# Norms of one group's queries and keys as two 64-column products, their inverse root on 256 columns, spread to 128 partitions by transfers

## The reference, cut to what matters

```python
def l2norm(t):
    return t / jnp.maximum(jnp.linalg.norm(t, axis=-1, keepdims=True), 1e-12)

def attn_layer(x, Wqkv, qs, ksc, Wo):
    qkv = x @ Wqkv
    q, k, v = ...                       # 16 heads of 64
    q = l2norm(q) * qs
    k = l2norm(k) * ksc
    q = q * cos * scale + rotate_half(q) * sin * scale
    k = k * cos * inv + rotate_half(k) * sin * inv
    out = local_attention(q, k, v)      # windows of 32 tokens, each sees itself and the one before
    return out @ Wo

for i in range(DEPTH):                  # DEPTH = 6
    x = attn_layer(shift_tokens(x), ...) + x
    x = ffn_layer(shift_tokens(x), ...) + x
```

## Time and profile before

| | |
|---|---|
| median of three runs | 1870.31 us |
| the profiled execution: its time | 1873.87 us |
| the profiled execution: its span | 1872.1 us |
| TensorE matmul busy | 1808.1 us (97%) |
| VectorE busy | 1535.6 us (82%) |
| ScalarE busy | 1456.2 us (78%) |
| GpSimd busy | 1359.4 us (73%) |
| granted TensorE clock, mean | 0.998 |

### The profile page before, as it was taken

How to read it: one execution, slowest core, us unless ns; L and a number is a source line. 1 busy time by engine, 2 the same in 40 slices (tenths; PEclk the granted TensorE clock), 3 DMA queues, 4 the chain that set the end, 5 groups by cost and what they waited for, 6 DMA issues and landing times.

```text
span 1872.1 us, 67927 instructions
## 1 busy us (share of the span) xinstructions
PE 1808.1 (97%) x26763; PEld 1370.4 (73%) x26763; DVE 1535.6 (82%) x3002; ACT 1456.2 (78%) x2976; POOL 1359.4 (73%) x1165
## 2 busy tenths in 40 slices
PE   6999998999999999999999999999999999999997
PEld 4777776777777777777777777777777777777774
DVE  5776777788889888888888888888888888888886
ACT  5766665678798888888887888778878878887884
POOL 3010023889889888888888898888888888888880
PEclk9999999999999999999999999999999999999999
DMA  3000001344343444334444434443344434444342
GB/s 111 1 1 0 0 25 28 91 114 116 104 110 100 112 113 111 97 103 110 114 112 104 105 102 115 113 107 101 103 106 122 112 98 103 111 104 103 98 103 69
DMA packets 200545, 171.01 MB, mean 91 GB/s; under 512 B 32400, under 2 KB 199480, under 8 KB 200248
## 3 DMA queue, kind: packets, MB, share of 16 engines
q1 hardware_dynamic: 200248, 166.89, 34.1%
HBM read 21.01 MB, written 1.05 MB: 12 GB/s over the span
## 4 chain that ended last, share of the span: by engine, by line
PE 61%; ACT 12%; DVE 11%; issue 7%; SPq 5%; POOL 4%; DMA 1%; ACTq 0%; DVEq 0%; POOLq 0%
PE bank L1011 6%; PE bank L1052 6%; PE bank L979 5%; PE pair_bank L1030 5%; PE bank L1062 4%; SPq L366 4%; PE bank L1114 3%; PE bank L1063 3%; PE bank L1064 3%; PE bank L1040 3%; PE bank L1136 3%; PE bank L897 2%; ACT sq L656 2%; DVE rot_v L1378 2%; PE bank L985 1%
## 5 line engine op out<-in xcount | busy, mean ns | idle before, releaser
L437 POOL TENSOR_TENSOR z_norm<-probs_t,z_raw 128x512 f32<-128x512 f32 x376 | 480.9, 1279 | 106.4 <-DVE probs_t L1459 104.2
L443 POOL TENSOR_TENSOR z_raw<-rot_u,rot_v 128x512 f32<-128x512 f32 x384 | 497.9, 1301 | 74.8 <-DVE rot_v L1378 72.0
L1377 DVE TENSOR_TENSOR rot_u<-bank,tabs 128x512 f32<-128x512 f32 x384 | 263.2, 685 | 175.8 <-ACT sq L656 174.6
L1062 PE MATMUL bank<-x_high,w_high 128*128 128x256 f32 x768 | 302.2, 394 | 0.0
L470 POOL TENSOR_TENSOR sqs<-sq 128x512 f32<-128x512 f32 x192 | 246.3, 1283 | 59.0 <-issue 57.9
L1378 DVE TENSOR_TENSOR rot_v<-bank,tabs 128x512 f32<-128x512 f32 x384 | 261.3, 681 | 0.0
L1052 PEld LDWEIGHTS bank<-probs_t,v_late 128*64 128x64 f32 x3072 | 155.0, 137 | 144.4 <-issue 144.4
L732 ACT ACTIVATE pair_bank<-pair_bank 128x512 f32<-128x512 f32 x192 | 111.7, 582 | 169.9 <-DVE pair_bank L1358 168.5
L656 ACT ACTIVATE sq<-bank 128x512 f32<-128x512 f32 x384 | 222.0, 593 | 24.2 <-PE bank L1064 17.7
L665 ACT ACTIVATE probs_t<-bank 64x512 f32<-64x512 f32 x340 | 200.9, 591 | 22.8 <-PE bank L1040 20.7
L1064 PE MATMUL bank<-x_low,w_high 128*128 128x256 f32 x768 | 216.4, 282 | 0.0
(11 more groups left out here) (190 smaller groups left out, 4538.6 us busy)
## 6 DMA issues: line engine op xcount, KB each, us to landing
zqk<-z_norm SPq DMA_DIRECT2D x1536, 64.0 KB, 2.1
v_late<-v_sb SPq DMA_DIRECT2D x192, 192.0 KB, 2.6
w_stage<-in_L_ffn_Wqkv SPq DMA_DIRECT2D x24, 384.0 KB, 3.6
v_late<-v_sb SPq DMA_DIRECT2D x192, 32.0 KB, 2.8
wo<-in_L_ffn_Wo SPq DMA_DIRECT2D x24, 128.0 KB, 2.4
w<-in_L_ffn_W SPq DMA_DIRECT2D x12, 170.5 KB, 3.1
z_norm<-in_L_attn_x SPq DMA_DIRECT2D x4, 256.0 KB, 5.3
out<-z_raw SPq DMA_DIRECT2D x4, 256.0 KB, 2.3
```

The source lines that it names most:

```text
L437: return pool.tensor_tensor(z_norm[:, parity, idx, :, :], rinv(m)[:, idx, :].unsqueeze(1).broadcast_to([P, 2, T]), z_raw[:, parity, idx, : ...
L443: pool.tensor_tensor(z_raw[:, parity, idx, :, :], rot_u[:, idx, :, :], rot_v[:, idx, ::-1, :], ALU.add).then_inc(S[mark], 1)
L1062: pe.matmul(dst, w_high[:, r, j, cols], x_high[:, odd, :], start=True, stop=False)
L1377: dve.tensor_tensor(rot_u[:, idx, :, :], src, tabs[:, 2 * idx, :, :], ALU.mult)
```

## The change

The matrix `blk` has 64 columns instead of 128, so that a head's sum comes out on 16 partitions. `norms` is two products of 256 columns, one for each column half of the array (`tile_position` (0, 0) and (0, 64)): the queries' norms land on partitions 0 to 63, the keys' on 64 to 127, in 256 columns. Logarithm, exponential and minimum run on 128x256. Four transfers then spread the rows to 128 partitions (`wide`): each row goes to two neighbouring partitions. GpSimd multiplies one slot later, with group s+2 in slot s instead of s+3, keys and queries directly one after the other, and in place: `rotated` writes `z`, `normalise` reads and writes it, and the transfers to `zqk` read it. There are four of those now, each of 64 partitions, with the two halves of a head interleaved.

```diff
-for _name, _n in (... ("blk", P), ...
+for _name, _n in (... ("blk", P // 2), ...
-    put("blk", i // 32 == np.arange(P)[None, :] // 32)
+    put("blk", i // 32 == np.arange(P // 2)[None, :] // 16)
...
-        z_raw = sb("z_raw", [P, 2, 2, 2, T])
-        z_norm = sb("z_norm", [P, 2, 2, 2, T])
+        z = sb("z", [P, G, 2, 2, T])
...
             def slot(s):                                                  # SyncE
-                if active(s, -2, GROUPS - 2):
-                    g = (s + 2) % G
-                    sp.wait_ge(S["zn_ready"], s + 3)
...
-                    for h in range(HG):
-                        for half in range(2):
-                            to = 64 * (h % 2) + 32 * half
-                            sp.dma_start(zqk[to:to + 32, g, :, h // 2, :], z_norm[32 * h:32 * h + 32, s % 2, :, half, :]).then_inc(S[f"z_in{g}"], 16)
                 if active(s, -3, GROUPS - 3):
...
+                    sp.wait_ge(S["bound_ready"], s + 4)
+                    after(sp, "zn_ready", s + 2)
+                    for idx in range(2):
+                        for k in range(2):
+                            sp.dma_start(wide(s + 3)[k:P:2, idx, :], rinv(s + 3)[64 * idx:64 * idx + 64, :]).then_inc(S["wide_in"], 16)
+                if active(s, -2, GROUPS - 2):
+                    g = (s + 2) % G
+                    sp.wait_ge(S["zn_ready"], s + 3)
...
+                    for pair in range(2):
+                        for half in range(2):
+                            sp.dma_start(zqk[half:P:2, g, :, pair, :], z[64 * pair:64 * pair + 64, g, :, half, :]).then_inc(S[f"z_in{g}"], 16)
...
             def slot(s):                                                  # GpSimd
...
                 if one:
-                    rotated(s + 4, s % 2, 1, "k_prod", "k_summed")
-                if two:
-                    pool.wait_ge(S["bound_ready"], s + 4)
-                    after(pool, f"z_in{(s + 1) % G}", 16 * 2 * HG * ((s + 1) // G + 1))
-                    pool.wait_ge(S["k_summed"], s + 4)
-                    normalise(s + 3, 1)
+                    rotated(s + 4, 1, "k_prod", "k_summed")
+                if near:
+                    pool.wait_ge(S["wide_in"], 16 * HG * (s + 3))
+                    pool.wait_ge(S["k_summed"], s + 3)
+                    normalise(s + 2, 1)
+                    pool.wait_ge(S["q_summed"], s + 3)
+                    normalise(s + 2, 0).then_inc(S["zn_ready"], 1)
...
-                if two:
-                    pool.wait_ge(S["q_summed"], s + 4)
-                    normalise(s + 3, 0).then_inc(S["zn_ready"], 1)
-                if one:
-                    rotated(s + 4, s % 2, 0, "q_prod", "q_summed")
+                    rotated(s + 4, 0, "q_prod", "q_summed")
...
-                    act.activation(ln_n(m), B_N[:, :].rearrange("p (a t) -> p a t", a=2), ACT.Ln, ...)
+                    act.activation(ln_n(m), B_N[:, 0:T], ACT.Ln, ...)
                     act.wait_ge(S["ln_done"], m + 1)
-                    after(act, "zn_ready", m)
+                    after(act, "wide_in", 16 * HG * m)
                     act.activation(rinv(m), ln_n(m), ACT.Exp, scale=-0.5).then_inc(S["rinv_ready"], 1)
...
-                pe.matmul(B_N[:, :], con("blk"), sqs[:, :, :]...).then_inc(S["n_done"], 1)
+                for idx in range(2):
+                    rows = slice(64 * idx, 64 * idx + 64)
+                    mm = pe.matmul(B_N[rows, 0:T], con("blk"), sqs[:, idx, :], start=True, stop=True, tile_position=(0, 64 * idx), skip_group_check=True)
+                mm.then_inc(S["n_done"], 1)
```

41 lines of the change are left out of this document (22 added, 19 removed).

## The result

The changed kernel takes 1912.52 us (median of 4 runs, 1907.82 to 1915.68) beside 1870.26 us of the kernel before on the same chip: a ratio of 1.0226, 95% interval 1.0214 to 1.0239. It is 42 us slower. The forecast was 1888 us (+18), with a range to 1912: the sign was right, the forecast shift was less than half of the measured one, and the time lies 0.5 us outside the range. They also show that the forecast's sum without that term comes close to the measured times partly by luck.

A forecast was written before the change was run, and what follows sets the result against it. The prediction took TensorE as the bound, other engines in places; 0 + 1.13 + 0.35 - 3 x 0.40 + 0.50 = 0.78 us a round, 18 us for 23 rounds, gave a median of 1888 us, range 1822 to 1912.

The forecast's parts named there:

- that term: Issues of transfers on SyncE, ten a slot before and after, which the forecast put at nothing.
- TensorE's gain: Norms as two side-by-side products of 256 columns: 0.40 us a slot, 74 us if TensorE bounds all eight slots.
- The minimum blocked by GpSimd: VectorE's minimum stands until GpSimd's product with the roots ends: 1.28 us instead of 0.42, 0.86 more.
- The first rival: Minimum goes ahead of GpSimd's product or between two without loss: -1.9 us a round, 1826 us; chance 0.20.
- I take nothing: SyncE's transfers to `zqk`: 7.2 or 8 us after the minimum fit into 9 us of room, so no cost.
- Slots 0 to 2: Slots that end when VectorE is ready; the blocked minimum shifts `hid` and the product waiting for it by 1.13 us.
- Slot 3: Minimum already blocked there before, 0.51 us of slack; shift of 0.35 us for this slot.
- The wait for the sum of squares at the norms of slot 6: GpSimd's key rotation, two products and sum in a row make TensorE wait 0.9 us: 0.50 for this slot.
- Slots 6 and 7: Slot 7: TensorE bounds it, -0.40 us; slot 6, counted from its own norms, also -0.40.
- The second rival: Block is there, but slots 3 and 6 have cover as TensorE is late: -0.47 us a round, 1859; chance 0.20.
- The third: Rival: transfers' landing grows by 1 us, windows of two slots start 0.5 late each: 1911 us; chance 0.08.
- The fourth: Rival: the array halves don't run side by side, 0.5 us a slot lost in slots 4 to 7: 1934; chance 0.02.

The follow-up runs named there:

- x13: Changed kernel, complete, with the bound moved into the logarithm's bias (no minimum on VectorE) and six SyncE issues a slot instead of ten: 1819.28 us, ratio 0.9716.
- x9: Kernel before, complete, with VectorE's minimum removed and its bound put into the logarithm's bias: 1853.33 us, ratio 0.9914.
- x17: x9 with half of the transfers to `zqk` left out (four of eight a slot), products in their early slot: 1845.94 us, ratio 0.9881.
- x1: Changed kernel with VectorE's minimum left out, its signal still given from the same place: 1843.88 us, ratio 0.9874.
- x10: Changed kernel, complete, with the bound moved into the logarithm's bias, SyncE and GpSimd waiting for the exponential directly: 1839.92 us, ratio 0.9859.
- x2: Changed kernel with GpSimd waiting again for the minimum before its products with the roots: 1861.05 us, ratio 0.9948.
- x3: Changed kernel without the four transfers that spread the roots; both products read the exponential's plane, so use roots of other rows: 1890.56 us, ratio 1.0107.
- x14: Changed kernel, complete, same bytes in six SyncE issues a slot instead of ten, the minimum kept: 1892.44 us, ratio 1.0112.
- x15: x7 with its four unread transfers cut to 8 columns, 2 KB each instead of 64 KB: 1909.07 us, ratio 1.0208.
- x7: x3 with four transfers of the same size issued again at the same place, into a plane nobody reads: 1912.96 us, ratio 1.0228.

## Why the forecast was right in part and wrong in size

**TensorE's gain**: right. 0.38 by the records, 0.40 in the forecast; slot 4, which TensorE bounds alone, is 0.41 shorter. The 74 us that it would be in all eight slots show in no run. x13 is 34 us under x9, and its six issues are a part of that (up to 7 us, by x17); TensorE still waits there, 17.5 us for the sum of squares and 16.9 us for `probs`.

**The minimum blocked by GpSimd**: right in mechanism and size. 1.27 us against 1.28, started 0.15 behind the product against 0.13; the forecast had 62 for it. Block and instruction together cost 69 us by x1 and 73 by x10, and the instruction was worth 17 already before (x9); the wait put back in x2 gives 51. The Trainium skill ("SBUF — State Buffer", section "Who interferes with whom") has it that DVE and GpSimd share a port pair as an exclusive lock, and that the one that issues first holds it for its whole instruction; 0.284 us alone (x2) and 1.27 us behind a product agree with that. The first rival, the minimum ahead of the product, is out.

**The step that failed: the transfers, "I take nothing".** The forecast counted ten issues of 0.64 us, 6.4 us a slot, and never set that beside the length of a slot; it set eight issues and a landing, 7.2 to 8 us, against a room of 9. Three things were wrong in it. The queue's ten issues have to be set beside the shortest slots: slot 0 had 6.77 us, and ten issues took 7.32, since one in ten or so takes 1 to 2 us. The landing at the end was 3.40, so the path from the minimum's end to the windows is 1033.16 to 1041.76, 8.6 us. And it began with a minimum that the block itself had made 0.86 late; the forecast's two terms lie on one path. TensorE's waits for these transfers came to 37.9 us between 400 and 1800 us (2.9 with six issues). The price is 22 us by x3 and 20 by x14, some 30 at full clock. Which of the two, the full queue or the longer path, costs more stays open. The earlier trace rows already had 5% of the chain on SyncE's queue, and I read over it.

The Trainium skill ("DMA: Bandwidth & Descriptors", section "Issuing engines are not separate DMA queues") says that the time a sequencer takes to initiate a DMA is usually small relative to the DMA itself. In this kernel it is not the transfer that one has to compare it with: 0.6 us of issue beside 2.6 of landing, but landings overlap and issues don't, and x15 costs almost as much as x7.

**A term that nobody had: the clock.** With the issues gone the measured times are 1890.6 (x3) and 1892.4 (x14) beside a forecast of 1888, and that looks like a proof of the rest of the sum. It is not. Some 12 to 16 us of both are the granted clock at half behind the waits in slot 2, for which the forecast has no term; at full clock they would be near 1875 to 1880, a shift of 5 to 10 us where 18 were forecast (an estimate from the lengths of slot 2 with and without the fall).

**The single slots.** Slots 0 to 2 lost 1.49 instead of 1.13. Slot 3 lost 0.11 instead of 0.35: there was more slack. The wait for the sum of squares at the norms of slot 6 is there, in 20 of 22 rounds, but it is 0.29 us a round where the forecast had 0.9; the row of slot 5 lost 0.21 (0.24 with six issues) instead of 0.50. Slots 6 and 7 should each have gained 0.40. With ten issues they lost 0.25 and gained 0.08: TensorE waits there for the transfers to `zqk` (0.20 and 0.11 us a round) and for ScalarE's `gate` (0.23 in each). With six issues slot 7 has its gain (-0.49), slot 6 only 0.09; what holds it stays open. So the sum of a round with SyncE relieved, +1.05 against +0.78, agrees by errors that nearly cancel.

**The second rival** (cover in slots 3 and 6) had a true core, since slots 3 and 6 lost less than forecast at the norms and at `hid`, but not its sign overall. **The third** (transfers that land later, 1911) had nearly the measured time; the landing grew by 0.5 us, not by 1, and it was the issues that cost. **The fourth** (the halves one after the other) is out: 0.48 us.

## What to carry to other kernels

Count the issues of each DMA queue against the shortest stage, not the mean, and ask how much lead the queue has: four of ten issues cost 7 us where their data is ready a stage ahead and 20 to 47 us where it is ready just in time. When a wait is removed, look for two engines that it kept apart; here one such wait, put back, was worth 51 us, and removing the instruction that it protected 73. A change that loses may be one obstacle away from winning: the whole change with six issues and no minimum is 34 us under the best form of the kernel before. And when an experiment lands on the forecast, look at the granted clock before taking it as a proof: here it hid some 12 to 16 us.

## What the runs showed of the hardware that I had not expected

- An issue of a transfer takes 0.59 to 0.62 us of SyncE in the median for 2 KB, 64 KB, 128 KB or 256 KB alike (x15, the changed kernel, x14). About one in ten takes 1 to 2 us; in the changed kernel four transfers of 128 KB in a row took 3.03 to 3.97.
- A transfer whose source reads each partition's row twice, from 64 partitions to 128, works in one issue (x14).
- Larger transfers land later, 2.1, 2.6 and 3.9 us for 64, 128 and 256 KB to `zqk`, and x14, with the slowest landing and the fewest issues, is faster than the changed kernel.
- Behind an idle time of TensorE of 2.2 us the granted clock fell from 2.4 to 1.2 GHz for 3.41 us in 12 of 16 cases (x14), which made the slot 1.35 us longer.
